# Row sums of blocks 1 to 7 from a second, row-wise copy of adj, in a two-layer graph kernel on one core

## What is computed

```python
def _L0_gnn_ref(h, adj, W_neigh, b_neigh, W_self, b_self):
    deg = jnp.sum(adj, axis=1, keepdims=True) + 1e-05
    h_neigh = (adj / deg) @ h
    return relu(h_neigh @ W_neigh.T + b_neigh + h @ W_self.T + b_self)

def _L1_gnn_ref(x, adj, W, b):
    rowsum = adj.sum(axis=1)
    d = jnp.where(rowsum > 0, rowsum ** (-0.5), 0.0)
    return relu((d[:, None] * adj * d[None, :]) @ x @ W + b)

x = _layernorm(x + _L0_gnn_ref(...), axis=-1)
x = _layernorm(x + _L1_gnn_ref(...), axis=-1)
```

## Time and profile before

| | us |
|---|---|
| median of 3 runs | 790.84 |
| lowest, highest | 790.61, 791.32 |
| the profiled execution, its own time | 791.16 |
| its span, first to last instruction | 789.4 |

### The profile page before, as it was taken

How to read it: one execution, slowest core, us unless ns; L and a number is a source line. 1 busy time by engine, 2 the same in 40 slices (tenths; PEclk the granted TensorE clock), 3 DMA queues, 4 the chain that set the end, 5 groups by cost and what they waited for, 6 DMA issues and landing times.

```text
span 789.4 us, 11269 instructions
## 1 busy us (share of the span) xinstructions
PE 779.0 (99%) x3789; PEld 650.5 (82%) x3789; DVE 585.2 (74%) x891; ACT 396.4 (50%) x550; POOL 0.4 (0%) x7
## 2 busy tenths in 40 slices
PE   9999999999999999999999999999999999999996
PEld 5778888888888888888888888888888888888886
DVE  5999999999899998999966554554546454554544
ACT  4564644646456464554554545354444544544452
POOL 0000000000000000000000000000000000000000
PEclk9999999999999999999999999999999999999998
DMA  8875574655646556465565656757575574757541
GB/s 318 290 265 188 190 254 169 218 191 187 231 163 234 186 186 239 159 239 187 180 233 186 211 196 189 239 179 234 168 245 178 182 241 166 236 183 240 186 143 47
DMA packets 54748, 160.93 MB, mean 204 GB/s; under 512 B 5057, under 2 KB 18753, under 8 KB 54721
## 3 DMA queue, kind: packets, MB, share of 16 engines
q1 hardware_dynamic: 46224, 152.06, 56.8%
q10 hardware_dynamic: 8496, 8.52, 3.3%
HBM read 152.17 MB, written 8.39 MB: 203 GB/s over the span
## 4 chain that ended last, share of the span: by engine, by line
PE 91%; DVE 6%; DMA 2%; issue 0%; ACT 0%; SPq 0%; DVEq 0%
PE ps_main L790 81%; PE ps_epi L714 8%; DVE lo L453 2%; DVE acc L634 2%; PE ps_main L812 1%; DMA raw<-adj_t 1%; DVE xs L453 1%; DMA xt_sb<-xt 1%; DVE st_lo L453 0%; PE ps_epi L822 0%; ACT hi L287 0%; PE ps_epi L736 0%; DVE acc L630 0%; DVE tt L483 0%; DVE stats L660 0%
## 5 line engine op out<-in xcount | busy, mean ns | idle before, releaser
L287 ACT ACTIVATE hi<-raw 128x1024 fp32r<-128x1024 f32 x254 | 269.0, 1060 | 303.7 <-PE ps_main L790 292.0
L453 DVE TENSOR_TENSOR lo<-raw,hi 128x1024 fp32r<-128x1024 f32 x254 | 309.9, 1220 | 122.3 <-ACT hi L287 122.1
L790 PE MATMUL ps_main<-hi,xs 128*128 128x512 f32 x1120 | 358.1, 390 | 2.0 <-DVE lo L453 2.0
L790 PE MATMUL ps_main<-hi,zs 128*128 128x512 f32 x880 | 277.9, 389 | 0.0
L790 PEld LDWEIGHTS ps_main<-hi,xs 128*128 128x128 f32 x1120 | 210.5, 188 | 47.1 <-issue 4.3
L790 PE MATMUL ps_main<-lo,xs 128*128 128x512 f32 x560 | 218.6, 390 | 0.0
L790 PEld LDWEIGHTS ps_main<-hi,zs 128*128 128x128 f32 x880 | 165.4, 188 | 33.8
L790 PE MATMUL ps_main<-lo,zs 128*128 128x512 f32 x440 | 171.6, 390 | 0.0
L634 DVE TENSOR_TENSOR acc<-acc,raw 128x1024 f32<-128x1024 f32 x112 | 135.9, 1213 | 0.0
L790 PEld LDWEIGHTS ps_main<-lo,xs 128*128 128x128 f32 x560 | 105.4, 188 | 19.4
L790 PEld LDWEIGHTS ps_main<-lo,zs 128*128 128x128 f32 x440 | 82.7, 188 | 15.8
(11 more groups left out here) (101 smaller groups left out, 383.1 us busy)
## 6 DMA issues: line engine op xcount, KB each, us to landing
raw<-adj_t SPq DMA_DIRECT2D x255, 512.0 KB, 3.3
res<-x_nat SPq DMA_DIRECT2D x11, 512.0 KB, 5.8
xt_sb<-xt SPq DMA_DIRECT2D x8, 512.0 KB, 5.1
x_scratch<-tt ACTq DMA_DIRECT2D x8, 512.0 KB, 5.1
res<-x_scratch SPq DMA_DIRECT2D x8, 512.0 KB, 6.1
out<-tt ACTq DMA_DIRECT2D x7, 512.0 KB, 6.5
tt<-x_nat SPq DMA_DIRECT2D x4, 512.0 KB, 5.9
raw<-adj_t SPq DMA_DIRECT2D x2, 256.0 KB, 4.3
```

The source lines that it names most:

```text
L287: return act.activation(dst, src, ACT.Copy)
L453: return dve.tensor_tensor(dst, src, hi_part.bitcast(f32), ALU.subtract)
L790: last = pe.matmul(ps[:, f, :], stationary(layer, part, jt, f), mov[:, slot(u), cols], start=(jt == 0 and i == 0), stop=(jt == JT - 1 and ...
```

## The change

For blocks 1 to 7 a second copy of `adj`, `rows`, is given in memory, laid out by rows: a piece is 128 rows x 1024 of their 4096 elements, 0.524 MB, and a block has 16 (4 row tiles x 4 pieces). GpSimd's queue loads them (line 319 of the changed kernel) into the two halves of `acc`, even pieces into the half for odd blocks, odd pieces into the other. ScalarE sums the even pieces by a copy with an accumulator (line 432), behind its `hi` of the same unit; VectorE sums the odd ones by a reduction (line 687), behind its `lo` of the same unit. Each writes one column of `row_parts`; at unit 4 of the next block VectorE adds the four columns of a row. The additions into `acc`, the folding, the bf16 parts and TensorE's 12 small matmuls are left for block 0 alone. SP's loads from unit 4 of block 1 on no longer wait for the additions. The loop of layer 0 covers blocks 2 to 5 now, and blocks 1, 6 and 7 are written out.

```diff
+        def row_part(parity, u):
+            return row_parts[:, parity, u // RQ, u % RQ:u % RQ + 1]
+        def row_piece(u):
+            return acc[:, 1 - u % 2, :]
...
-                        if layer == 0 or (is_first(b) and u < RING):
+                        if layer == 0 and (is_first(b) or (is_second(b) and u < RING)):
                             sp.wait_ge(acc_done, g0 + (u - RING + 1))
...
+            def load_rows(b, u):
+                if is_second(b) and u == 0:
+                    pool.wait_ge(unit_done, WHOLE)
+                    wait_x_split(pool, 0)
+                elif is_second(b) and u == 1:
+                    pool.wait_ge(rs_summed, 1)
+                else:
+                    pool.wait_ge(rows_read[u % 2], (b - 1) * (NU // 2) + u // 2)
+                pool.dma_start(row_piece(u), rows_in[b, u]).then_inc(rows_full[u % 2], 16)
...
                     if epi is not None:
                         after_unit(*epi, 1 - parity, u)
+                    if layer == 0 and not is_first(b) and u % 2 == 0:
+                        act.wait_ge(rows_full[0], ((b - 1) * (NU // 2) + (u // 2 + 1)) * 16)
+                        act.activation(row_piece(u), row_piece(u), ACT.Copy,
+                                       accum_out=row_part(parity, u)).then_inc(rows_read[0], 1)
...
-                    if layer == 0:
+                    if layer == 0 and is_first(b):
                         a = acc[:, parity, :]
...
+                    if layer == 0 and not is_first(b) and u % 2 == 1:
+                        dve.wait_ge(rows_full[1], ((b - 1) * (NU // 2) + (u // 2 + 1)) * 16)
+                        dve.tensor_reduce(row_part(parity, u), row_piece(u), AX.X, ALU.add).then_inc(rows_read[1], 1)
...
-                if u == 1 and layer == 0:
+                if u == 1 and layer == 0 and by_acc(e):
-                    pe.wait_ge(part3_ready, e + 1)
+                    pe.wait_ge(part3_ready, 1)
...
+        "rows": np.ascontiguousarray(adj.reshape(NB, TB, P, RQ, UW).transpose(0, 1, 3, 2, 4)).reshape(NB, NU, P, UW),
```

More of the change, by code:

```diff
@@ L38 @@
 ZOWN = JT - TB
+RQ = NU // TB
 HB = IB // 2
@@ L45, with build @@
 TINY = 1e-35
-def build(nc, x_nat, xt_in, adj_in, wn_in, bn_in, ws_in, bs_in, w1_in, b1_in, out):
+def build(nc, x_nat, xt_in, adj_in, rows_in, wn_in, bn_in, ws_in, bs_in, w1_in, b1_in, out):
     f32 = mybir.dt.float32
@@ L118, in build @@
         acc_folded = sem("acc_folded")
+        rows_full = [sem(f"rows_full{i}") for i in range(2)]
+        rows_read = [sem(f"rows_read{i}") for i in range(2)]
         part1_ready, rest_ready = sem("part1_ready"), sem("rest_ready")
@@ L142, in is_first, with is_second @@
             return isinstance(b, int) and b == 0
+        def is_second(b):
+            return isinstance(b, int) and b == 1
         def xt_unit(b):
@@ L189, in layers @@
         def layers(eng, one_block, last_epilogue):
[L192 to L197, removed]
+            one_block(0, 0, 0, None)
+            one_block(0, 1, 1, (0, 0))
+            with eng.Fori(2, NB - 2, 2) as b:
+                one_block(0, b, 0, (0, b - 1))
+                one_block(0, b + 1, 1, (0, b))
+            one_block(0, NB - 2, 0, (0, NB - 3))
+            one_block(0, NB - 1, 1, (0, NB - 2))
+            one_block(1, 0, 0, (0, NB - 1))
+            with eng.Fori(1, NB - 1, 2) as b:
+                one_block(1, b, 1, (1, b - 1))
+                one_block(1, b + 1, 0, (1, b))
+            one_block(1, NB - 1, 1, (1, NB - 2))
             last_epilogue((1, NB - 1))
@@ L281, in _ @@
             pool.memset(marks[:, 0:1], 0.0).then_inc(tt_stored, 16)
+            def load_rows(b, u):
[7 more added lines that the diff above has]
+                pool.dma_start(row_piece(u), rows_in[b, u]).then_inc(rows_full[u % 2], 16)
+            for u in range(NU):
+                load_rows(1, u)
+            with pool.Fori(2, NB) as b:
+                for u in range(NU):
+                    load_rows(b, u)
         @block.scalar
@@ L322, in after_unit @@
                 n = e + layer * NB
-                if layer == 0 and v == 0:
+                if layer == 0 and by_acc(e) and v == 0:
                     act.wait_ge(acc_folded, e + 1)
                     act.activation(sum_part(0, parity), acc[:, parity, 0:IB], ACT.Copy).then_inc(part1_ready, 1)
-                if layer == 0 and v == 1:
+                if layer == 0 and by_acc(e) and v == 1:
                     act.wait_ge(rest_ready, e + 1)
@@ L461, in begin, with degrees @@
                 links[0], links[1] = 0, e * LINKS[layer] + (NB * LINKS[0] if layer else 0)
[L463 to L468, removed]
+            def degrees(e, parity, p):
+                if p == 0 and by_acc(e):
+                    dve.wait_ge(rs_summed, 1)
+                    link(dve.tensor_copy(row_sums[:, :], ps_epi[:, TB - 1, 0:TB]))
+                elif p == 0:
+                    dve.wait_ge(rows_read[0], e * (NU // 2))
+                    dve.wait_ge(rows_read[1], e * (NU // 2))
+                    link(dve.tensor_reduce(row_sums[:, :], row_parts[:, parity, :, :], AX.X, ALU.add))
                 if p == 1:
-                    dve.tensor_scalar(pos[:, :], sums_of_rows, 0.0, None, ALU.is_gt)
+                    linked()
+                    link(dve.tensor_scalar(rdeg[:, :], row_sums[:, :], EPS_DEG, None, ALU.add))
+                    dve.tensor_scalar(pos[:, :], row_sums[:, :], 0.0, None, ALU.is_gt)
+                if p == 2:
                     linked()
                     link(dve.reciprocal(rdeg[:, :], rdeg[:, :]))
-                if p == 2:
-                    dve.tensor_scalar(root_in[:, TB:2 * TB], sums_of_rows, TINY, None, ALU.max)\
-                       .then_inc(rs_copied, 1)
+                    dve.tensor_scalar(root_in[:, TB:2 * TB], row_sums[:, :], TINY, None, ALU.max).then_inc(rs_copied, 1)
             def scale_product(layer, n, t):
@@ L552, in epilogue @@
                 rest = acc[:, parity, 0:IB]
-                if (v, p) == (0, 1) and layer == 0:
+                if (v, p) == (0, 1) and layer == 0 and by_acc(e):
                     dve.wait_ge(part1_ready, e + 1)
                     dve.tensor_tensor(rest, rest, sum_part(0, parity), ALU.subtract).then_inc(rest_ready, 1)
-                if (v, p) == (1, 1) and layer == 0:
+                if (v, p) == (1, 1) and layer == 0 and by_acc(e):
                     dve.wait_ge(part2_ready, e + 1)
@@ L742, in epilogue @@
                         pe.wait_ge(stl_ready, n + 1)
-                    if t == TB - 1 and layer == 0:
-                        pe.wait_ge(rs_copied, e + 1)
+                    if t == TB - 1 and layer == 0 and by_acc(e):
+                        pe.wait_ge(rs_copied, 1)
                     product(ps_epi[:, t, 0:F], slice(t * P, (t + 1) * P),
```

13 lines of the change are left out of this document (8 added, 5 removed).

## The result

The changed kernel takes **874.05 us** (median of 4 runs, 872.74 to 875.85) against 790.73 of the kernel before on the same chip: ratio 1.1054, with a 95% interval from 1.1041 to 1.1067. It is 83 us slower, where 13 were forecast, and lies far above the forecast range, 798 to 822. The profiled execution took 875.85 us, with a span of 874.2.

The account below looks back on a forecast made before the run. TensorE was taken to bound the kernel from about 45 us on. Seam delay 12.2 plus clock 3.5 minus small matmuls 2.8 gave +12.9 us on 791.16: 804 us, range 798 to 822.

Parts of the forecast that it names:

- What leaves TensorE: Seven blocks lose their 12 small matmuls on TensorE, 0.40 us each: 2.8 us gained.
- The seam: Between blocks 0 and 1, row pieces wait for buffers still in use: product 12.2 us late, plus 3.5 us of clock.
- The spells: TensorE's two idle times at the start of block 1, before unit 1 and behind the row sums: 3.4 and 8.8 us.
- The clock: TensorE's granted clock falls after each idle spell in block 1, costing 1.3 and 2.2 us, together 3.5.
- Blocks 2 to 7: A buffer's round, landing 4.7 plus pass 1.25 us, fits in two units, 6.2 us: loss taken as 0.
- The 3.3 us of slack in `st_lo`: In a steady block `st_lo` is 3.3 us early, which a late piece eats first.
- The rival of the round trip: Landing plus pass paces blocks 2 to 7, from 4.95 us landing; 13 us more at 5.2, 817 us; chance 0.18.
- The rival of the DMA rate: DMA engines can't carry the 371 GB/s a block then needs: 12 us more, 816 us; chance 0.13.
- The price of a load on GpSimd's queue: At the seam, piece 1's load taken as 4.1 us, between `raw` loads alone, 3.3, and with others, 4.7.
- The seam covered: Rival: `st_lo` still ends before the product of block 1 wants it, only the gain stays: 788 us; chance 0.05.

Follow-up runs that it names:

- experiment 1: The changed kernel with each row piece's load cut to 64 of its 1024 columns, all waits kept: 797.95 us.
- experiment 4: The changed kernel with four row buffers instead of two, and `zs` moved to the end of the local memory: 797.71 us.
- experiment 5: The changed kernel with four row buffers, as in experiment 4, but `zs` at its old address: 790.18 us, ratio 0.9995.
- experiment 10: As experiment 5, but in blocks 1 to 5 all four buffers lie where `zs` is filled only in blocks 6 and 7: 787.99 us, ratio 0.9965.
- experiment 2: The kernel before, with GpSimd also loading 96 row pieces of blocks 1 to 6 that nobody reads, and `zs` moved: 793.02 us.
- experiment 6: The kernel before, without row loads, with `zs` alone moved to the end of the local memory: 798.57 us.

## Why the prediction was wrong

- **What leaves TensorE, 0.40 us a block**: right. Wherever the pieces came in time a block fell from 49.84 to 49.44 us (experiments 1, 4, 5, 10).
- **The seam**: right, in its steps and nearly in its sum. Predicted for block 1 were 12.2 + 3.5 = +15.7 us, measured +16.9. The spells were 4.96 and 8.59 us against 3.4 and 8.8. Piece 0 took 5.9 us from its issue to the pass rather than 4.7, as `raw` and `xt` were under way; piece 1 took 3.55, below my 4.1. The clock fell at both spells, as forecast, and cost 1.7 and 1.8 us against 1.3 and 2.2: the same sum, 3.5, from two parts that were each off.
- **Blocks 2 to 7: "At 4.7 us landing that is 5.95, which fits with 0.2 us to spare … So I take 0 here"**: this step failed, by 67 us net, and 70 against the forecast 49.44 us a block. Two of its terms were wrong. The round was a landing and a pass, with no hand-over: in truth 0.66 us pass between the end of a pass and the next load on GpSimd's queue, and 0.04 between landing and pass, less 0.10 since the pass was shorter than costed (1.15). So 0.60 us was missing, and at 4.7 us landing a round is 6.55, not 5.95: 0.37 too long, 48 times, 18 us. The landing was the larger one: 4.7 was read from six `raw` loads in block 0, and ScalarE's pieces took 5.75 on average: 1.05 x 48 = 50 us. Together 68, measured 67.7 by the distance of the passes ((7.59 - 6.18) x 48).
- **The 3.3 us of slack in `st_lo`**: it can absorb one late piece. It can't absorb a round that is too long each time, since the lateness of one round is the start of the next.
- **The rival of the round trip** had the mechanism, with 0.18, and a wrong price. Its threshold, a landing of 4.95 us, was in truth 6.18 - 0.04 - 1.15 - 0.66 = 4.33 us, under the 4.7 that I held for normal. With that threshold it was the likeliest case. Even its far end, 42 us for 5.8 us landing, lacked the hand-over.
- **The rival of the DMA rate** fell: 373 GB/s for 200 us with TensorE full (experiment 10). The Trainium skill, "DMA: Bandwidth & Descriptors", section on specifications, gives one core about 358 GB/s from HBM; the trace of experiment 10 doesn't agree, the measured 373 lies above. Its section on bandwidth has 425 GB/s for one core alone with 16 MB, which was the figure to weigh against it. The changed kernel itself moved only 304, because it waited.
- **The price of a load on GpSimd's queue.** Piece 1 at the seam, with only piece 2 behind it, took 3.55 us from issue to pass; in company a piece took 5.75 us to land. The Trainium skill, "DMA: Bandwidth & Descriptors", section on the anatomy of a DMA on the GpSimd path, gives 2.0 us plus the bytes at 436 GB/s, an estimate of 3.2 us, which is near the first of these and far from the second.
- **The seam covered**: what speaks against it was right, it needed other buffers (experiment 10).

What sets the landing time in company stays open beyond this: it grew with what was in flight, from 3.5 us with one other piece (the seam) over 5.3 (median, two buffers, 304 GB/s) to 6.9 (four buffers, 373 GB/s), and with the bunch at a block's end. Here more loads in flight made each slower and the stream faster.

## What to carry to other kernels

A buffer that is refilled when its reader is done costs landing + wait for the reader + pass + hand-over to the queue, each round. Take the landing from loads in the company that the change will create, put every hand-over in, and compare with the time of a round; if it is even near, add buffers, since four slots made 7 us harmless where two failed at 5.1. When no engine and no DMA is full and the chain of waits is a third DMA, suspect such a round before you suspect bandwidth. Where a new stream borrows a buffer, look at who still holds it at the start, and check that moving tensors to make room hasn't changed the address of a matmul's operand.

## What was unexpected of the hardware

- The start address of the stationary operand `zs` changed the pace of the matmuls: from start to start 227 ns at a multiple of 128 bytes, 229 at 64 bytes past one (experiment 2), 233 to 234 at 96 bytes past one (experiments 4 and 6), 8 us over layer 1.
- From the end of ScalarE's or VectorE's pass to the start of the load on GpSimd's queue 0.64 us pass in a loop and 0.29 where the loads are written out, on SP's queue 0.03 (when SP is free); and GpSimd is busy for 0.53 us with each load, SP for 0.33.
- A store of x1 that landed after 13.5 us, and `raw` loads after 6.5, cost nothing (experiment 2): landing time matters only against the number of slots.
